# Graph attention and a mixture of experts on one core: who splits W1, the order of the lead-in, an unrolled expert half with a third W1 buffer, and another order at the end

## The reference

```
x1  = x + elu(softmax(where(adj > 0, leaky_relu(si + sj), -9e15)) @ Wh)   # Wh = layernorm(x) @ W.T, si = Wh@a1, sj = Wh@a2
x2  = layernorm(x1)
routing = softmax of (mean of x2 over the batch's 512 rows) @ Wr + br, rescaled to capacity; top 2 of 8 experts per batch
y   = sum over the 2 experts of  w_k * (gelu(x2 @ W1[e] + b1[e]) @ W2[e] + b2[e])
out = x1 + layernorm(y + x2) * gamma + beta
```

## Time and profile before

| | us |
|---|---|
| median of 3 runs | 291.31 (290.0 to 292.25) |
| the profiled execution | 289.25 |
| its span | 287.2 |
| PE busy in the span | 256.7 (89%) |
| DVE busy | 234.9 (82%) |
| ACT busy | 224.5 (78%) |
| POOL busy | 151.9 (53%) |

### The profile page before, as it was taken

How to read it: one execution, slowest core, us unless ns; L and a number is a source line. 1 busy time by engine, 2 the same in 40 slices (tenths; PEclk the granted TensorE clock), 3 DMA queues, 4 the chain that set the end, 5 groups by cost and what they waited for, 6 DMA issues and landing times.

```text
span 287.2 us, 6697 instructions
## 1 busy us (share of the span) xinstructions
PE 256.7 (89%) x1872; PEld 227.9 (79%) x1872; DVE 234.9 (82%) x669; ACT 224.5 (78%) x513; POOL 151.9 (53%) x231
## 2 busy tenths in 40 slices
PE   7869998999878989999988699599999999999964
PEld 3449987888778878899978447499999999999954
DVE  5588999999999999999998564627777678777756
ACT  2447889998988899999999749288878797988370
POOL 4442197778988897786548312013344333334534
PEclk9988999999999999999999869999999999999997
DMA  6999356653366246441000014933454454454122
GB/s 86 232 242 184 83 91 106 113 100 66 59 108 105 55 65 111 73 54 24 2 3 0 0 47 128 311 132 117 153 166 162 149 182 166 164 183 164 55 73 74
DMA packets 40670, 31.50 MB, mean 110 GB/s; under 512 B 2401, under 2 KB 36609, under 8 KB 40641
## 3 DMA queue, kind: packets, MB, share of 16 engines
q1 hardware_dynamic: 31936, 21.72, 23.3%
q0 software_dynamic: 8704, 9.45, 22.0%
HBM read 27.48 MB, written 4.20 MB: 110 GB/s over the span
## 4 chain that ended last, share of the span: by engine, by line
PE 41%; ACT 6%; issue 3%; SPq 3%; DMA 2%; DVE 2%; POOL 1%; POOLq 0%; DVEq 0%; ACTq 0%
PE banks L1412 16%; PE banks L1259 5%; PE banks L1397 4%; PE banks L1399 4%; PE banks L1398 4%; DMA w_pair<-w_parts 2%; ACT leaky L990 2%; PE banks L1244 2%; PE banks L1236 1%; PE banks L1210 1%; PE banks L1432 1%; ACT leaky L1149 1%; ACT x2t_all L1030 1%; SPq L326 1%; SPq L335 1%
## 5 line engine op out<-in xcount | busy, mean ns | idle before, releaser
L1259 PE MATMUL banks<-whx,prob_t 128*128 128x129 f32 x512 | 67.9, 277 | 2.8 <-ACT h_att L1000 2.5
L1259 PEld LDWEIGHTS banks<-whx,prob_t 128*128 128x128 f32 x512 | 61.8, 192 | 5.7 <-issue 5.7
L421 POOL TENSOR_SCALAR x_all<-x_all,rstd,nb 128x128 f32<-128x128 f32 x56 | 42.3, 766 | 2.9 <-POOL nb L410 2.9
L1244 PE MATMUL banks<-ident,logit 128*128 128x128 f32 x256 | 37.1, 278 | 4.8 <-DVE logit L577 4.0
L1025 ACT ACTIVATE prob_t<-banks 128x512 f32<-128x512 f32 x64 | 38.3, 640 | 3.7 <-PE banks L1244 3.6
L487 POOL TENSOR_SCALAR veps<-mv 128x4 f32<-128x4 f32 x15 | 7.1, 472 | 60.7 <-DVE mv L857 60.7
L1139 ACT ACTIVATE logit<-logit,nb,rstd 128x128 f32<-128x128 f32 x60 | 24.8, 484 | 17.3 <-POOL nb L492 17.3
L1244 PEld LDWEIGHTS banks<-ident,logit 128*128 128x128 f32 x256 | 29.9, 143 | 6.4 <-DVE logit L577 6.2
L404 POOL TENSOR_TENSOR rstd<-var,minus_half 128x8 f32<-128x8 f32 (+1 forms) x20 | 33.6, 1679 | 0.4
L1412 PEld LDWEIGHTS banks<-w2s,masked_even 128*128 128x128 f32 x256 | 29.7, 192 | 0.5
L1397 PE MATMUL banks<-x2t_hi,w_pair 128*128 128x512 f32 x64 | 26.8, 418 | 3.5 <-DMA w_pair<-w_parts 3.5
(11 more groups left out here) (151 smaller groups left out, 569.8 us busy)
## 6 DMA issues: line engine op xcount, KB each, us to landing
adj_sb<-in_adj_dram POOLq DMA_DIRECT2D x16, 512.0 KB, 7.1
w_pair<-w_parts SPq DMA_DIRECT2D x30, 256.0 KB, 2.3
x_all<-in_x_dram SPq DMA_DIRECT2D x16, 256.0 KB, 2.8
w2r<-in_L_ffn_W_dram SPq DMA_DIRECT2D x32, 128.0 KB, 2.1
out_dram<-prob_t SPq DMA_DIRECT2D x15, 256.0 KB, 2.3
w_parts<-in_L_ffn_W_dram SPq DMA_DIRECT2D x1, 1024.0 KB, 8.3
b_mix<-b_spread POOLq DMA_DIRECT2D x1, 768.0 KB, 6.7
b_mix<-b_spread POOLq DMA_DIRECT2D x1, 256.0 KB, 4.3
```

The lines of the kernel that those rows point to most:

```text
L421: nc.gpsimd.tensor_scalar(x_all[:, b, tile], x1_all[:, b, tile], rstd12[c % 4][:, 1, t:t + 1], nb2[c % 2][:, t:t + 1], ALU.mult, ALU.add). ...
L1244: last = nc.tensor.transpose(lt_ps[t % 2][:, c * P:(c + 1) * P], logit[:, t, c * P:(c + 1) * P], ident[:])
L1259: last = nc.tensor.matmul(into[:, 0:D + 1], prob_t[:, t, c * P:(c + 1) * P], whx[b % 3][:, c, 2:WHX], start=(c == 0), stop=(c == T - 1))
```

## The change

The change has seven parts. W1's low parts are made on VectorE instead of GpSimd: one piece before `residual_pos(14)`, two after `scale_x2_last`, one in the router behind `r_weight`. The lead-in of VectorE, ScalarE and TensorE is in another order. Near the end of the attention half ScalarE's `copy_x2t(13)` stands behind `last_normalize(3)`, and TensorE's filler is 11, 3, 2, 7 instead of 6, 2, 2, 7. In the expert half there is no loop and no `waits_met`; there are three `w1_pair` buffers; SyncE's list has W1 of batch 2 ahead of W2 of batch 1; b2's rows come back in three DMAs (batches 0 and 1, 2 to 4, 5 to 15), the last of them issued after `norm3(0)`. At the end TensorE does `hidden_part(15)` before `out_part(14)`, ScalarE does `apply_gelu(15)` before `scale_w2(15)`, `norm_z(13)` and `norm_z(14)`, and VectorE does `scale_gamma(13)` and `finish(13)` before `sum_z(14)`.

```diff
-        w1_pair = [sb(f"w1_pair{i}", [P, TOP_K, 2, F], F32R) for i in range(2)]
+        w1_pair = [sb(f"w1_pair{i}", [P, TOP_K, 2, F], F32R) for i in range(3)]
...
-        WARM = (6, 2, 2, 7)
-        B2_FIRST = 4
+        WARM = (11, 3, 2, 7)
+        B2_PARTS = (0, 2, 5, B)
...
             def load_w1(b):
-                par = b % 2
-                if b >= 2:
-                    sp.wait_ge(s_hid_ps, KC * (b - 1))
+                if b >= 3:
+                    sp.wait_ge(s_hid_ps, KC * (b - 2))
...
             sp.wait_ge(s_w1lo, 4)
-            sp.wait_ge(s_x2t_ps, B)
             sp.wait_ge(s_idx, 1)
             load_w1(1)
             load_w2(0)
+            load_w1(2)
             load_w2(1)
-            load_w1(2)
-            load_w2(2)
 
             for n in range(B):
-                if 1 <= n < B - 2:
-                    load_w1(n + 2)
+                if n + 3 < B:
+                    load_w1(n + 3)
+                if n + 2 < B:
                     load_w2(n + 2)
...
             for n in range(B):
                 step(n)
-                if 5 <= n < 9:
-                    split_w1_lo(n - 5)
...
+            load_b2(0)
+            load_b2(1)
...
+            def step2(n):
+                if 0 <= n <= B - 1:
+                    norm3(n)
+                if n == 0:
+                    load_b2(2)
...
+            def split_w1_lo(part):
+                es = slice(part * E // 4, (part + 1) * E // 4)
+                dve.wait_ge(s_w1hi, part + 1)
+                nc.vector.tensor_tensor(w1_parts[:, es, 1, :], w1_parts[:, es, 1, :].bitcast(F32),
+                                        w1_parts[:, es, 0, :].bitcast(F32), ALU.subtract).then_inc(s_w1lo, 1)
...
+            logits(B - 1, 2)
+            logits(B - 1, 3)
+            split_w1_lo(0)
+            residual_pos(END)
...
             for t in range(T):
                 scale_x2_last(t)
+            split_w1_lo(1)
+            split_w1_lo(2)
...
             router_steps["weighted"] = rc[0]
+            split_w1_lo(3)
             dve.wait_ge(s_rps, 3)
...
-            sum_z(0, END)
-            stats3(0, END)
-            aggregate3(0, END)
-            scale_gamma(0, END - 1)
-            finish(0, END - 1)
+            scale_gamma(END - 1)
+            finish(END - 1)
+            sum_z(END)
+            stats3(END)
+            aggregate3(END)
             last_stats(0)
-            scale_gamma(0, END)
             last_stats(1)
+            scale_gamma(END)
...
-            copy_x2t(B - 3)
             last_normalize(2)
             last_normalize(3)
+            copy_x2t(B - 3)
...
-            pipeline(act, step2, 0, B - 3, 4, 2)
-            scale_w2(0, B - 1)
-            norm_z(0, END - 1)
-            apply_gelu(0, B - 1)
-            norm_z(0, END)
+            for n in range(B - 2):
+                step2(n)
+            apply_gelu(B - 1)
+            scale_w2(B - 1)
+            norm_z(END - 1)
+            norm_z(END)
...
-            keep_busy(8)
+            keep_busy(5)
             transpose_logits(0, 0)
+            keep_busy(3, lt_ps[1])
+            project(2)
             transpose_logits(0, 1)
-            project(2)
...
-            pipeline(pe, step2, 0, B - 3, 4, 0)
-            out_part(0, B - 2)
-            hidden_part(0, B - 1)
+            for n in range(B - 2):
+                step2(n)
+            hidden_part(B - 1)
+            out_part(B - 2)
             last_out_part()
```

More of the change, by code:

```diff
@@ L672, in _, with split_x2t_lo @@
             shift_max(1)
+            stats1(3)
+            shift_row(1)
+            shift_low(1)
+            shift_high(1)
             make_mask(2)
-            shift_row(1)
-            for n in range(1, B):
-                step(n)
-            def split_x2t_lo(half, n):
-                b, h, par = batch_at(half, n)
-                if past(half, b, 2):
+            stats1(4)
+            stats1(5)
+            masked_max(2, 0)
+            logits(1, 0)
+            logits(1, 1)
+            invert_sums(0)
+            masked_max(2, 1)
+            logits(1, 2)
+            masked_max(2, 2)
+            logits(1, 3)
+            masked_max(2, 3)
+            residual_pos(0)
+            shift_max(2)
+            make_mask(3)
+            shift_row(2)
+            for n in range(2, B - 1):
+                step(n)
+            residual_neg(END - 1)
+            shift_low(B - 1)
+            stats2(END - 1)
+            shift_high(B - 1)
+            logits(B - 1, 0)
+            logits(B - 1, 1)
+            invert_sums(END)
+            logits(B - 1, 2)
+            logits(B - 1, 3)
+            split_w1_lo(0)
+            residual_pos(END)
+            def split_x2t_lo(b):
+                par = b % 2
+                if b >= 2:
                     dve.wait_ge(s_hid_ps, KC * (b - 1))
@@ L948, in _ @@
             gamma_tile(1)
[L949 removed]
+            finish(END)
             last_stats(2)
```

261 lines of the change are left out of this document (116 added, 145 removed).

## The result

The changed kernel takes 280.06 us (median of 4 runs, 279.45 to 282.64); the kernel before, run beside it, 290.76 (4 runs, 290.0 to 292.25). The ratio is 0.964, with a 95% interval of 0.957 to 0.972: 3.6% faster. The forecast was 283.2, range 280.2 to 287.0: the direction is right, the time lies at the range's low edge, 0.14 under it; as a share of the kernel before it lies inside (0.964, range 280.2 / 291.31 = 0.962 to 0.985).

A forecast was written before the change was run, and what follows sets the result against it. VectorE was taken to bound the attention half, TensorE the expert half, the norm chain the last 20 us. Terms 3.9 + 0.75 + 2.0 + 3.4 + 0 - 2.0 = 8.05 off 289.25: 281.2, against the median 283.2; range 280.2 to 287.0.

The forecast's parts named there:

- Low parts off GpSimd: Attention half: four steps fall from 9.72 to 8.75 us, 3.9 gained; low bound 2.8.
- rival 1: Attention half does not follow VectorE down; ScalarE or TensorE sets the steps, 2.5 to 3 lost: 286; chance 0.13.
- Low parts on VectorE: End of attention half and router: four W1 pieces mostly fill idle time; piece 3 costs 0.20; uncovered, all 2.8.
- The term taken for it into the low bound: End of attention half: piece 0 could be late by one GpSimd instruction, up to 0.7.
- The end of the attention half and the router: ScalarE's copy moved, more filler: 0.95 idle goes, clock stays near 1.00; +0.75 with piece 3, bounds -0.7 and +1.2.
- Lead-in: New order removes two VectorE idles, 0.91 and 1.31; 2.0 gained, bounds 0.9 and 2.3.
- SyncE's list and the third buffer: Start of expert half: W1 of batch 2 goes out earlier, TensorE's 3.50 idle goes; 3.4 gained, bounds 1.5 and 3.5.
- Rival 2: Start of expert half: W1 still comes late, half of the 3.4 is lost: 285; chance 0.08.
- Unrolling: Expert half: writing out the looped batches changes nothing, as TensorE has no gap there; 0.
- Rival 4: Written-out expert half starves TensorE in ten batches; a wait of 1.2 per batch gives 295; chance 0.04.
- The end: Last batches: new order ends 3.4 later, shorter `nb` gives 0.35, missing markers 1.0; sum -2.0, bounds -3.4 and -0.5.
- Rival 3: The end costs nothing if GpSimd and ScalarE without markers let `sum_z(14)` start by 275: 281.3; chance 0.09.

The follow-up runs named there:

- experiment 7: The changed kernel with TensorE's filler 6, 2, 2, 7 instead of 11, 3, 2, 7: 280.03 us, ratio 0.968.
- experiment 4: The changed kernel with the lead-in of VectorE, ScalarE and TensorE in the old order: 282.68 us, ratio 0.990.
- experiment 10: The changed kernel with the whole old end on VectorE, ScalarE and TensorE, without marker instructions: 278.99 us, ratio 0.972.
- the last pair: The changed kernel with four more filler matmuls on TensorE in the router: 280.55 us with the new end, 277.87 with the old end order.

## Why the prediction was right, and where it was off

- **Low parts off GpSimd, 3.9 forecast:** 3.78 measured, and 3.81 with the kernel that undoes it alone. The steps stand at 8.78 rather than 8.75. ScalarE's slack was enough, so rival 1 fell.
- **Low parts on VectorE, 0.20 forecast:** 0.33 (0.06 + 0.27). Piece 0 was not held up: 0.69. The term taken for it into the low bound was not needed. It is GpSimd that gave way: its scaling that starts at 147.02, before the piece at 147.34, took 1.25, where the shortest of them takes 0.45, and VectorE was still in batch 15's logits (146.00 to 147.42) when that row began; so the engine whose row starts first isn't always the one that goes on. All four took 3.50, where the same four took 3.07 before (at 153.19), and nobody waited for them.
- **The end of the attention half and the router, 0.75 with piece 3:** 1.39 - 0.13 = 1.26. The copy's order gave 1.01 (0.95 forecast). The filler's share in the argument (the column sums would eat up the 0.95 without it) is not shown: in experiment 7 the sums ran at the high level all the same. Of the 0.38 that is left up to `x_sum`, 0.30 lies behind the start of the last pair of `scale_x2_last` (1.80 to `x_sum`, 2.10 before). There VectorE had waited 1.43 for column sums of 1.71 at a clock of 0.50; now they take 0.95, and W1's two pieces end last. So the clock was worth some 0.3 here, in this pair of profiles; no experiment shows it.
- **Lead-in, 2.0:** 1.81 in the profile, 1.95 by the experiment. One idle of 0.32 stays. The prediction put both idles down to the order of work alone; with the old order the granted clock is 0.70 ahead of the longer one as well (experiment 4), so this part of the mechanism is open. Mask(0) came 0.61 earlier as well; that was not forecast, and since mask(0) starts anywhere from 10.27 to 10.71 in the variants, and at 11.02 in the one profile of before, part of it is scatter.
- **SyncE's list and the third buffer, 3.4:** 3.77. Undone one by one, the order gives back 1.17 and b2's parts 1.53; the third buffer was not tried alone, and the three need not add up. Rival 2 (W1 still late) would have shown an idle at `hidden_part(2)`; there is none. The fear that W2 of batch 1 would be next was right in kind: it is what comes late when b2's parts are undone.
- **Unrolling, 0:** a batch takes 6.33 (`out_part(0)` at 170.54, `out_part(13)` at 252.78), and in the loop it took 6.33, too (`out_part(4)` at 207.00, `out_part(13)` at 263.94), TensorE busy throughout in both. Rival 4 fell with it. No variant put the loop back. The Trainium skill (Runtime: NRT & Kernel Launch, Instruction fetch mechanics) calls a taken branch out of the code that is already fetched a cause of a fetch stall; no row before or after shows one here, and the looped batches, with branches, were as full as these.
- **The end, -2.0:** -1.53, of which the order is -2.4 and the rest +0.9. The forecast of the parts was -3.4 for the order, +0.35 for a shorter `nb` and +1.0 for the markers. By the runs the order was over-priced by 1.0, `nb` brought nothing in the old end (0.65), and of the +0.9 some 0.45 goes with TensorE's clock in the last batch; 0.44 at most is left for the markers (experiment 10). So the total came close because two errors met. In the chain the difference lies in three places: `scale_gamma(13)` started 11.08 after `out_part(13)` (263.86 - 252.78; 11.65 before), `sum_z(14)` to `scale_gamma(14)` took 5.75 where 6.6 was counted, and from there to the end it was 4.63 where 5.0 was (5.65 less 0.5 is 5.15, a slip of 0.15 in the sum). Rival 3 (the end costs nothing) fell.

The terms sum to 8.05, the measurement to 9.63: the 1.58 are 0.61 of mask(0), 0.51 at the end of the attention half, 0.37 in the expert half and 0.47 at the end, less 0.19, 0.12 and 0.07. The other 1.5 us between 283.2 and 280.06 is no step of the kernel: the profiled execution of before stood 2.06 below its median, that of after 0.61 below its own, and the forecast carried the 2.06 over. So no term missed by more than 0.51, and the waits that the prediction named were the ones that went: the hold-up by GpSimd, the copy on ScalarE and the late W1 are shown by experiments, the two idles of the lead-in with the clock's share open. That the whole is as close as it is owes something to luck, with mask(0) and the clock of single executions on one side and the two errors at the end on the other. The stated spread was rough as well: the bounds of the terms, taken as independent, give 1.6 us to the fast side and 3.2 to the slow side and not 2 either way, so the low edge of 280.2 leaned on the scatter of the runs.

Without its part on the last batches' order the change would have been worth 2.4 more by the profiles, 2.7 by the medians of the last pair.

## What to carry to other kernels

Where a short instruction is far longer in a few steps than in the others, look at what the other engine was reading at that moment: such a hold-up counts as busy time and appears in no wait. A filler or a reordering that fills idle time is worth something only on the engine that bounds the stretch; the same low clock cost 0 to 0.35 in the router and 3.0 at the start of the expert half. At a kernel's end, don't let the chain of a later batch stand behind the finish of an earlier one that is itself still waiting: here `out_part(14)` was done at 262.85, and `sum_z(14)` stood behind a `scale_gamma(13)` that could start only at 263.86. And before you read a gain from two profiles, compare the granted clock in the same stretch of both.

## What the runs showed that was not expected

- The granted clock fell to 0.50 for the first 5 us of the expert half in some executions of a program whose others kept 1.00 there, with some 2.4 us idle in the 7 us before in both cases; with four more fillers the runs scattered as before.
- GpSimd's 128x4 `nb` takes 0.20 when VectorE is idle beside it (269.08 in the changed kernel) and took 0.55 and 0.65 (experiment 10) beside VectorE's `finish(13)`, which has two inputs, and ended when that did: the hold-up works in both directions.
